# A three-step change to a fused graph-network kernel: store slots, scatter spacing and tile-number loads

## Time and profile before

| What | Value |
|---|---|
| median of 3 runs | 3692.08 us |
| lowest and highest | 3691.84 and 3708.81 us |
| the profiled execution's own time | 3690.83 us |
| its span | 3688.8 us |
| mean granted TensorE clock | 0.790 |
| busy: PE 69%, DVE 62%, ACT 39%, POOL 30% | of the span |
| HBM traffic | 443.97 MB read, 185.52 MB written |

### The profile page before, as it was taken

The page is one execution under the profiler, slowest core; times in us unless marked ns, Lnnn a source line. Parts: engine busy times, 40 slices in busy tenths (PEclk is TensorE's granted clock), DMA queues, the critical chain, the costliest instruction groups (busy, mean ns, idle before and its releaser), DMA issues.

```text
span 3688.8 us, 41851 instructions
## 1 busy us (share of the span) xinstructions
PE 2561.8 (69%) x12402; PEld 2077.5 (56%) x12402; DVE 2288.3 (62%) x4379; ACT 1451.6 (39%) x3050; POOL 1099.4 (30%) x878
## 2 busy tenths in 40 slices
PE   4678714555555536666477777979999999925998
PEld 3522203554555524454366666459888988924786
DVE  4979926888888887877322222354565576626776
ACT  2278813444454410000233333544433434423765
POOL 0016776666666666777200000000000000051000
PEclk9788855555555558888698888979999999967999
DMA  9982225666666655554587777006546645340887
GB/s 373 378 307 27 26 21 155 176 182 184 188 186 188 185 128 141 138 136 105 159 257 230 240 238 216 26 26 185 171 127 172 194 125 169 114 99 8 300 313 265
DMA packets 332245, 632.29 MB, mean 171 GB/s; under 512 B 93155, under 2 KB 206556, under 8 KB 325372
## 3 DMA queue, kind: packets, MB, share of 16 engines
q1 hardware_dynamic: 240350, 550.88, 45.9%
q0 software_dynamic: 78464, 58.39, 10.4%
q10 hardware_dynamic: 13214, 20.35, 1.6%
HBM read 443.97 MB, written 185.52 MB: 171 GB/s over the span
## 4 chain that ended last, share of the span: by engine, by line
PE 31%; DMA 8%; DVE 6%; issue 3%; ACT 3%; SPq 1%; POOL 1%; another core or an unknown queue 0%; DVEq 0%; ACTq 0%
PE banks L1196 25%; DMA weights<-reg 6%; PE banks L1141 2%; DMA ring<-pairs 2%; PE banks L1168 2%; PE banks L1120 1%; ACT reg L996 1%; POOL pairs L798 1%; SPq L712 0%; ACT reg L860 0%; DVE reg L1943 0%; DVE stats L1412 0%; ACT reg L1021 0%; DVE lhs_r L1742 0%; DVE reg L1435 0%
## 5 line engine op out<-in xcount | busy, mean ns | idle before, releaser
L1196 PE MATMUL banks<-rows_r,lhs_r 128*128 128x448 f32 x3850 | 1037.9, 391 | 48.0 <-DVE wts L1853 10.9
L1196 PEld LDWEIGHTS banks<-rows_r,lhs_r 128*128 128x128 f32 x3850 | 756.1, 201 | 135.0 <-DVE att_low L601 23.9
L798 POOL DMA_INDIRECT pairs<-wts x391 | 626.3, 1602 | 501.4 <-DMA weights<-ring 258.5
L1284 PE MATMUL banks<-lhs_r,oT 128*128 x416 | 203.5, 489 | 424.9 <-issue 329.8
L603 DVE SCALAR_TENSOR_TENSOR ring_r<-ring,dinv,rows_r 128x896 fp32r<-128x896 f32 (+1 forms) x300 | 303.4, 1033 | 302.9 <-ACT rows_r L589 302.8
L806 POOL DMA_INDIRECT reg<-tab_p,w x416 | 402.5, 968 | 244.9 <-issue 146.2
L836 POOL DMA_INDIRECT el<-tab_l,base_i x25 | 24.8, 991 | 1481.7 <-DMA tab_l<-reg 1474.4
L589 ACT ACTIVATE rows_r<-ring,dinv 128x896 fp32r<-128x896 f32 (+1 forms) x300 | 284.6, 950 | 393.0 <-PE banks L1196 376.1
L1284 PEld LDWEIGHTS banks<-lhs_r,oT 128*128 128x128 f32 x416 | 132.8, 319 | 437.5 <-issue 437.3
L1323 PE MATMUL banks<-reg 128*128 128x256 f32 x832 | 252.5, 471 | 146.2 <-DVE reg L1734 139.4
L599 DVE TENSOR_TENSOR rows_r<-ring,rows_r 128x448 fp32r<-128x448 f32 x175 | 108.7, 625 | 394.1 <-ACT rows_r L585 394.1
(11 more groups left out here) (256 smaller groups left out, 4432.4 us busy)
## 6 DMA issues: line engine op xcount, KB each, us to landing
ring<-weights SPq DMA_DIRECT2D x225, 448.0 KB, 3.4
ring<-pairs SPq DMA_DIRECT2D x200, 448.0 KB, 4.8
pairs<-ring SPq DMA_DIRECT2D x25, 3136.0 KB, 25.6
ring<-pairs SPq DMA_DIRECT2D x75, 896.0 KB, 5.5
zbuf<-reg SPq DMA_DIRECT2D x208, 256.0 KB
reg<-zbuf SPq DMA_DIRECT2D x52, 1024.0 KB
weights<-reg SPq DMA_DIRECT2D x84, 384.0 KB, 4.8
ring<-weights SPq DMA_DIRECT2D x75, 224.0 KB, 3.3
```

Source lines behind the costliest of these rows:

```text
L798: pool.indirect_dma_start(pairs, bass.IndirectOffsetOnAxis(ap=ix_c[:, k:k + 1], axis=0), vals[:, k, :], None, compute_op=ALU.add).then_inc ...
L1196: m = pe.matmul(bank[:, 0:BLK], lhs[part], rows[:, c:c + BLK], start=first, stop=last)
L1284: m = pe.matmul(ps[4 + q % 2][:, k % 2 * H:(k % 2 + 1) * H], oT[q // 4 % 2][:, k % 8 * P:(k % 8 + 1) * P], part[:, bass.ds(tiles[k], 1), : ...
```

## The change

Three parts. (1) Four staging slots instead of two: the third lies where `conv` will be loaded, the fourth over `w1`; the loads of `conv` and of the attention vectors therefore come behind `wait_turned`. (2) `C_EVERY` goes from 8 to 4: one scatter after every four gathers, 104 in the z stage and not 52. (3) Tile numbers are loaded four at a time, on VectorE at the same place, on TensorE for the next pass, behind the second pair of the preceding one.

```diff
-C_EVERY = 8
+C_EVERY = 4
+TURN = 4
...
-        turned = [view(RF + k * 8 * P, 4, 2 * P) for k in range(2)]
...
+        turned = [view(RF, 4, 2 * P), view(RF + 8 * P, 4, 2 * P), weight(CONV, 4, 2 * P),
+                  w1_flat.rearrange("p (a b) -> p a b", a=4)]
...
-        turn_stored = [sem(f"turn_stored{k}") for k in range(2)]
+        turn_stored = [sem(f"turn_stored{k}") for k in range(TURN)]
...
-            return pair_no[q] % 2
+            return pair_no[q] % TURN
...
-            for k in range(2):
-                eng.wait_ge(turn_stored[k], 32 * len(range(k, n_pairs, 2)))
+            for k in range(TURN):
+                eng.wait_ge(turn_stored[k], 32 * len(range(k, n_pairs, TURN)))
...
                 if pi == 1:
+                    wait_turned(sp)
+                    sp.dma_start(attn[:, 0, :], attn_l...).then_inc(gat_loaded, 16)
+                    sp.dma_start(attn[:, 1, :], attn_r...).then_inc(gat_loaded, 16)
                     sp.dma_start(conv[:, :, :], ...).then_inc(conv_loaded, 16)
-                    wait_turned(sp)
...
                 stream(pi)
-                if pi == 0:
-                    sp.wait_ge(filled, number["Q", (12,)] + 1)
-                    sp.dma_start(attn[:, 0, :], attn_l...).then_inc(gat_loaded, 16)
-                    sp.dma_start(attn[:, 1, :], attn_r...).then_inc(gat_loaded, 16)
...
-                    wait(act, turn_stored[k], 32 * (pair_no[q] // 2))
+                    wait(act, turn_stored[k], 32 * (pair_no[q] // TURN))
...
+            def load_tiles(i):
+
+                for k in range(8 * i, 8 * i + 8, 4):
+                    tiles[k:k + 4] = nc.values_load_multi_w_load_instructions(
+                        tile_ix[0:1, k:k + 4], engines=[pe.engine], min_val=0, max_val=NT - 1)[1]
+
+            load_tiles(0)
...
                 if q % 4 == 0:
                     pe.wait_ge(oT_ready, q // 4 + 1)
-                    tiles[2 * q:2 * q + 8] = [pe.value_load(tile_ix[0:1, k:k + 1], min_val=0, max_val=NT - 1) for k in range(2 * q, 2 * q + 8)]
...
                 for q in range(4 * i, 4 * i + 4):
                     add_q(q)
+                    if q % 4 == 1 and i + 1 < NPASS:
+                        load_tiles(i + 1)
...
-                tiles = [v.value_load(tile_ix[0:1, k:k + 1], min_val=0, max_val=NT - 1) for k in range(8 * i, 8 * i + 8)]
+                tiles = []
+                for k in range(8 * i, 8 * i + 8, 4):
+                    tiles += nc.values_load_multi_w_load_instructions(
+                        tile_ix[0:1, k:k + 4], engines=[v.engine], min_val=0, max_val=NT - 1)[1]
```

More of the change, by code:

```diff
@@ L393, in gnn_kernel @@
         assert 10 * NCH <= CONV
+        turned = [view(RF, 4, 2 * P), view(RF + 8 * P, 4, 2 * P), weight(CONV, 4, 2 * P),
+                  w1_flat.rearrange("p (a b) -> p a b", a=4)]
+        assert len(turned) == TURN
         ix_c = wts[:, CONV:CONV + NCH].bitcast(I32)
@@ L718, in stream @@
                 if pi == 1:
+                    wait_turned(sp)
+                    sp.dma_start(attn[:, 0, :], attn_l.rearrange("h d -> (h d)").unsqueeze(0).to_broadcast([P, H])).then_inc(gat_loaded, 16)
+                    sp.dma_start(attn[:, 1, :], attn_r.rearrange("h d -> (h d)").unsqueeze(0).to_broadcast([P, H])).then_inc(gat_loaded, 16)
                     sp.dma_start(conv[:, :, :], conv_w.rearrange("l (j p) n -> p (l j) n", p=P)).then_inc(conv_loaded, 16)
-                    wait_turned(sp)
                 for q in range(FIRST[pi] + (RING if pi == 0 else 0), FIRST[pi + 1]):
@@ L748, in _ @@
                 stream(pi)
-                if pi == 0:
-                    sp.wait_ge(filled, number["Q", (12,)] + 1)
-                    sp.dma_start(attn[:, 0, :], attn_l.rearrange("h d -> (h d)").unsqueeze(0).to_broadcast([P, H])).then_inc(gat_loaded, 16)
-                    sp.dma_start(attn[:, 1, :], attn_r.rearrange("h d -> (h d)").unsqueeze(0).to_broadcast([P, H])).then_inc(gat_loaded, 16)
             for s in range(NSPLIT):
```

## The result

The changed kernel took 3460.53 us (median of 4 runs, 3452.95 to 3468.24); beside it the kernel before took 3695.32 us (median of 4, 3691.84 to 3708.81). The ratio is 0.9358, 95% interval 0.9322 to 0.9394: 235 us less by the medians. The profiled execution took 3466.51 us (span 3464.7), 224.3 less than that of before. The forecast was 3492, 200 us less, within 3440 to 3580. The total held; two of its four terms did not, and their errors have opposite signs.

What follows compares the result with a forecast made beforehand. The prediction took latency, the wait for stores to land before slots are refilled, to bound pass 0. Its terms, 106 + 97 - 3 = 200 us off the profiled 3690.8, gave 3491, 3492 as a median, range 3440 to 3580.

Steps and rivals of the forecast that it cites:

- Pass 0: Pass 0 with four staging slots: the wait for stores goes, 414 us against 511.5, a gain of 97 us.
- at 100% that is 377 us, 2.23 us for each of 169 units: Pass 0: lower bound for its loads and stores, from 116 MB moved at 76.9% DMA share over 490 us.
- the transfers do better, as in pass 4: Rival for pass 0: 2.1 us a unit instead of 2.35, the whole kernel taking 3450 us; chance 8%.
- the stop that causes them goes: z stage: TensorE's 6.02 us stop per pass vanishes, so POOL bounds the stage at 737 us, gain 10 us.
- POOL's waits of today stay: Rival for the z stage: it takes 849 us instead of 737, the whole kernel 3604 us; chance 8%.
- The register loads: Message stage: tile numbers loaded four at a time hide behind VectorE's work, gain 73 us.
- the lower price: Message stage: one load of 0.301 us brings four registers, so eight tile numbers take 2.8 us, all hidden.
- The scatters behind the gathers: After the z stage: 155 scatters at 2.263 us each take 351 us, where 207 took 468.5.
- The message stage now ends last, with 14 us to spare for POOL: Before pass 0: VectorE's last add at 1669, POOL's last scatter landed at 1655, first product at 1682, gain 106 us.
- three signs by which the prediction called itself wrong: POOL still ends last, the gather stage is over 760 us, or pass 0 stays over 455 us.
- The seam: After pass 0: attention vectors load behind the last store's landing, a loss of 3 us.
- The slower rival: z stage: scatters clog the software queue, gathers land late, stage 1073 us, the whole kernel 3828 us; chance 3%.

## Why the prediction was right in its total, and where its steps failed

**What bounds the kernel.** Right: the landing of the stores was the latency of pass 0, and with four slots it left the chain. Taken alone it gives 180 us.

**Pass 0: the term was mis-sized,** 97 us forecast, 175 measured. The step that failed is "at 100% that is 377 us, 2.23 us for each of 169 units". The time that packets take isn't a fixed price: 67656 packets took 76.9% of 490 us, 377 us, in the kernel before. With the slots alone the same stretch of work, 1809 to 2129, has this row:

```profile
q1 hardware_dynamic: 67632, 116.75, 101.1%
```

67632 packets in 101.1% of 320 us, 324 us: a seventh less each. The busy share of a queue that stops and starts can't be scaled to 100% for a lower bound. The other lower bound, 1.89 us a unit from pass 4's 364 GB/s, was the right one: a unit takes 336.9 / 175 = 1.93 us at 357 GB/s. The forecast leant on the mix of this stage because it was the nearest row, and its own rival, "the transfers do better, as in pass 4", happened, further than its 2.1 us. TensorE isn't far from being the next bound: busy 311 of 337 us at a clock of 0.97. Its busy time fell from 372 us with the same products: with fewer stops the granted clock rose from 0.85 to 0.97, so it ran more often at 2.4 GHz. The Trainium skill, page "Trainium Architecture — The Big Picture", section "What this means for kernel authors", gives about 360 GB/s of HBM bandwidth for one core; by that rule the 0.686 MB of a unit would take 1.91 us, an estimate. The trace agrees, with 357 GB/s.

**The z stage: the step "the stop that causes them goes" failed.** 737 us were forecast, 790 measured, where the same text drew its line at 760. POOL's own time came as said (739 against 732). The loads alone gained 16 us (747 to 731), as the stop of TensorE went: the waits charged to its product fell from 58.4 to 11.2 us. But the remote waits rose in its place, from 50.4 to 107.8 us (each over the whole run). What is late next had been a row of the same line before (47.7 us in the stage), and the prediction leaves it out: it subtracted one wait and took VectorE to be free. The added scatters then cost 58 us (731 to 790), where the forecast had room for 6 beyond what the loads alone have; VectorE's remote waits rose with them by 25 us and its waits for the product by 29. Its rival, "POOL's waits of today stay", is as near as the forecast. POOL still waited for VectorE, 53.1 us and not 98.7, so the stage stands about halfway between the forecast and that rival's 849.

**The register loads: right,** 83 us against 73. Four registers come in one access of 0.34 us, as the lower price had it, and the passes recur every 5.98 us; of the 10 us of idle time that the forecast kept some 5 are there (311 - 306.4). The Trainium skill's figure of some 200 ns for each register (page "Runtime: NRT & Kernel Launch", section "Instruction fetch mechanics") isn't borne out: three more registers cost 40 ns together, 340 against 301.

**The scatters behind the gathers: nearly right.** 155 took (245.2 + 123.5) / 155 = 2.38 us each, not 2.263: 369 us against 351.

**Which chain ends last: wrong.** "The message stage now ends last, with 14 us to spare for POOL" missed by the z stage, since that shifts POOL's end one for one: its last scatter began at 1720.9, 9 us behind VectorE's last add. The front gained 53 us and not 106. With 54 us more in the z stage (last gather at 1353 and not 1299) and 18 in the tail the forecast's own sum puts the end of the scatters at 1655 + 54 + 18 = 1727, and the first product comes at 1735. Of the three signs by which the prediction called itself wrong two came true: POOL still ends last, and the gather stage is over 760 us.

**The seam: right.** VectorE waits 5.32 us for the attention vectors where it had waited 2.94; from the end of pass 0 to the end the kernel takes 3 us longer (1389.4 to 1392.7), as forecast.

**The sum.** 53 + 175 - 3 = 225 us in the trace, for 106 + 97 - 3 = 200. An error of 53 us in the front was more than made up by one of 78 in pass 0. That the total came within 32 us of 3492 is luck: had pass 0 taken the 414 us of the forecast, the total would have come near 3540. It would still have been in the range, but the range was drawn without a grown z stage.

**The chances.** The slower rival, a clogged software queue, didn't come: beside the first gather VectorE waits for one only once more, 1.5 us (74.7 - 73.2). But the spacing alone does make the kernel slower, by 29 us, by another way than that rival's: a longer z stage in front of a message stage that ends last. The chance of 3% was given for the three parts together, and these never came near it.

## What to carry to other kernels

Where two engines' chains meet at one point, compute both ends after every single part of a change: a part that shortens only one can be worth nothing or less alone (0.998, 1.008 here) and 60 us with its partner. When a wait disappears, read what else the same line waited for before, and set the gain by what is left. Don't scale the busy share of the DMA engines to 100% to get a transfer's floor when the stage has stops in it; take the rate of a stage that is full.

## What the hardware showed that had not been expected

- **A load of several registers costs hardly more than one:** 0.34 us for four against 0.30, on both engines. TensorE's operation behind each number takes 146 ns, VectorE's 183.
- **Packets take less time in a stream that never stops:** the same 67.6 thousand packets of pass 0 took 377 us of engine time at a share of 77%, and 324 at 101%. Why a stopping stream makes packets longer wasn't tried.
- **Signals of TensorE that come late,** by 7 to 8 us in the stop shown, about once in a group of cells, with every engine idle but POOL. In the kernel before, too, waits of this kind are there. Four experiments on TensorE's work didn't lower their sum (133 us; 136 to 160 in the four); it rises with the number of scatters among the gathers (108, 133 and 182 us at 52, 104 and 138 with the loads in fours). The cause is open.
- **One long scatter.** Scatters take 1.55 us beside the adds of the messages. The one that runs while VectorE adds two halves of the sums in SBUF takes 6.50. VectorE's timeline of the changed kernel, with that addition:

```profile
1712.31 6.83 DVE L1749 TENSOR_TENSOR reg<-reg 128x6400 f32<-128x6400 f32 x1
```

POOL's timeline beside it:

```profile
1712.20 1.55 POOL L799 DMA_INDIRECT pairs<-wts  x1 [0.30 <-issue]
1714.05 6.50 POOL L799 DMA_INDIRECT pairs<-wts  x1 [0.30 <-issue]
1720.86 1.80 POOL L799 DMA_INDIRECT pairs<-wts  x1 [0.30 <-issue]
```

It lies on the path here, since POOL ends last: 5 us. The Trainium skill, page "SBUF — State Buffer", section "Who interferes with whom", says that a VectorE instruction with both inputs in SBUF contends with a GpSimd instruction that reads SBUF. The traces fit that. The experiments moved the sum, and the long scatter moved with it; with the loads alone it stands 57 us earlier than in the change:

```profile
1653.51 6.83 DVE L1748 TENSOR_TENSOR reg<-reg 128x6400 f32<-128x6400 f32 x1
```

```profile
1657.02 4.73 POOL L798 DMA_INDIRECT pairs<-wts  x1 [2.85 <-issue]
```

In eleven of the twelve kernels one scatter beside the sum takes 4.7 to 7.8 us, and it ends 1.4 us behind the sum each time, wherever it began. With the spacing alone no scatter is left beside the sum, and none there is long. The subtraction of 128x6400 elements that makes the low part of q (L1617, 390.47 to 397.29 in the changed kernel), also with both inputs in SBUF, has such a scatter beside it too, 7.61 us from 391.13. The adds of the messages have one input in PSUM, and beside them a scatter keeps its 1.55 us.
